# Attention loops of a language-model tower: the turn of the probabilities placed ahead of the V products on TensorE

## What is computed

```python
# banded, four times
idx = jnp.arange(nc)[:, None] * W + jnp.arange(3 * W)[None, :]
scores = jnp.einsum('bhcqd,bhckd->bhcqk', qc, kb) / jnp.sqrt(jnp.asarray(d, q.dtype))
scores = jnp.where(allowed, scores, jnp.asarray(-1000000000.0, scores.dtype))
probs = jax.nn.softmax(scores, axis=-1)
out = jnp.einsum('bhcqk,bhckd->bhcqd', probs, vb)
...
# full, once
attn = jnp.einsum('bhqd,bhkd->bhqk', q, k) * SCALE
attn = jax.nn.softmax(attn, axis=-1)
out = jnp.einsum('bhqk,bhkd->bhqd', attn, v)
```

## Time and profile before

| what | value |
|---|---|
| median of three runs | 1809.26 us |
| the profiled execution, its own time | 1813.13 us |
| its span, first to last instruction | 1811.3 us |
| mean granted TensorE clock | 0.902 |
| busy: TensorE, VectorE, ScalarE, GpSimd | 81%, 68%, 54%, 45% |
| banded loops (four) | 52 to 210, 300.5 to 445, 535.5 to 682, 775 to 921 us |
| full loop | 1334 to 1487 us |

### The profile page before, as it was taken

One profiled execution on the slowest core, in us unless ns is written; L12 is line 12 of the kernel. 1 busy time (PEld: TensorE's weight loads), 2 busy tenths in 40 slices (PEclk: granted clock), 3 DMA queues, 4 the chain that ended last, 5 costly groups with the idle time before them and its releaser, 6 DMA issues.

```text
span 1811.3 us, 39511 instructions
## 1 busy us (share of the span) xinstructions
PE 1465.9 (81%) x13098; PEld 1256.1 (69%) x13098; DVE 1236.5 (68%) x3514; ACT 980.9 (54%) x2393; POOL 815.2 (45%) x1175
## 2 busy tenths in 40 slices
PE   2789799997998888988989488669478887499991
PEld 2578677786777777877778377269457666499991
DVE  6878876889768896688976722434478886444444
ACT  1578635887348883378843133245258872055550
POOL 7786235773347733378523200145365511145540
PEclk9799999999999999999999678579789996599996
DMA  4644004470026530174800000167345501267765
GB/s 114 163 89 106 1 1 123 105 145 11 1 62 146 115 60 1 25 182 89 226 2 1 14 1 1 47 207 244 115 97 119 102 2 47 102 198 243 239 199 182
DMA packets 144278, 177.87 MB, mean 98 GB/s; under 512 B 22096, under 2 KB 106128, under 8 KB 143952
## 3 DMA queue, kind: packets, MB, share of 16 engines
q1 hardware_dynamic: 136784, 158.18, 34.0%
q0 software_dynamic: 7296, 17.18, 2.8%
HBM read 132.96 MB, written 42.34 MB: 97 GB/s over the span
## 4 chain that ended last, share of the span: by engine, by line
PE 53%; DVE 23%; issue 8%; POOL 8%; DMA 4%; ACT 3%; SPq 1%; POOLq 0%; DVEq 0%; ACTq 0%
PE bank L1498 7%; PE bank L663 7%; DVE ptl L821 4%; PE bank L575 4%; DVE neg_max L814 3%; PE bank L427 3%; PE bank L445 2%; PE bank L1484 2%; PE bank L447 2%; PE bank L446 2%; PE bank L449 2%; PE bank L448 2%; DVE xx L788 2%; PE bank L540 2%; DVE row_b L821 1%
## 5 line engine op out<-in xcount | busy, mean ns | idle before, releaser
L703 ACT ACTIVATE prob<-bank,neg_max 128x192 f32<-128x192 f32 (+1 forms) x960 | 412.6, 440 | 117.5 <-DVE neg_max L814 108.9
L814 DVE TENSOR_REDUCE neg_max<-bank 128x2 f32<-128x384 f32 (+1 forms) x480 | 272.2, 569 | 70.6 <-PE bank L540 69.9
L575 PE MATMUL bank<-ident,prob 128*128 128x128 f32 x1536 | 272.1, 290 | 48.3 <-DVE ptl L821 36.1
L716 ACT ACTIVATE pth<-bank 128x384 f16<-128x384 f32 (+1 forms) x480 | 245.9, 512 | 5.7 <-PE bank L575 5.6
L821 DVE TENSOR_TENSOR ptl<-bank,pth 128x384 f16<-128x384 f32 (+1 forms) x352 | 204.5, 581 | 10.5 <-ACT pth L716 10.0
L575 PEld LDWEIGHTS bank<-ident,prob 128*128 128x128 f32 x1536 | 161.7, 142 | 65.0 <-DVE ptl L821 47.6
L670 ACT ACTIVATE xx<-bank 128x256 fp32r<-128x256 f32 x256 | 96.3, 390 | 176.1 <-PE bank L427 172.6
L540 PE MATMUL bank<-kx,qx 96*128 96x192 bf16 (+1 forms) x960 | 166.8, 255 | 1.4 <-DVE xx L788 1.1
L754 ACT ACTIVATE fbuf<-bank,b 128x512 f32<-128x512 f32 x96 | 66.0, 687 | 165.0 <-PE bank L449 165.0
L596 PE MATMUL bank<-v,pth 128*128 128x33 bf16 x1152 | 137.8, 179 | 21.5 <-DVE ptl L821 18.5
L663 PE MATMUL bank<-w,fbuf 128*128 128x192 f32 x768 | 140.7, 326 | 1.9 <-DVE h L914 1.9
(11 more groups left out here) (304 smaller groups left out, 4644.7 us busy)
## 6 DMA issues: line engine op xcount, KB each, us to landing
xn<-in_e_seg SPq DMA_DIRECT2D x34, 768.0 KB, 6.7
w<-in_e_w SPq DMA_DIRECT2D x23, 576.0 KB, 4.3
qk_rows<-fbuf SPq DMA_DIRECT2D x128, 96.0 KB, 2.3
qx<-qk_rows SPq DMA_DIRECT2D x35, 288.0 KB, 4.1
kx<-qk_rows SPq DMA_DIRECT2D x35, 288.0 KB, 5.9
qk_rows<-w SPq DMA_DIRECT2D x80, 96.0 KB, 2.3
qx<-qk_rows SPq DMA_DIRECT2D x35, 192.0 KB, 4.7
kx<-qk_rows SPq DMA_DIRECT2D x35, 192.0 KB, 5.4
```

The costliest lines, as they stand in the source:

```text
L575: last = nc.tensor.transpose(bank[BT[p % 2]][:, c * P:c * P + P], probs_at(p, banded, c * P, P), ident[:, :])
L703: nc.scalar.activation(probs_at(p, banded, qt * n, n), scores_at(p, n)[:, qt, :], ACT.Exp, bias=neg_max[:, b % 2, hd, qt:qt + 1], scale=1. ...
L716: nc.scalar.activation(high_at(p, banded), bank[BT[p % 2]][:, 0:n], ACT.Copy).then_inc(hi_ready.sem, 1)
L814: nc.vector.tensor_reduce(neg_max[:, b % 2, hd, :], scores_at(p, D if banded else S), AX.X, ALU.max, negate=True).then_inc(max_ready.sem, 1)
```

## The change

In every turn of the attention loops the turn of pair p-3 is now issued directly behind the scores of pair p, and the V products of the older pair behind the turn, ahead of `pe_step`. All four banded loops and the full loop go through this function. Nothing else is different: the waits, the buffers and the other engines' programs are the same.

```diff
             for p in range(PAIRS + behind(banded)):
                 if p < PAIRS:
                     pe_scores(pe, it, p, banded)
-                if p >= behind(banded):
-                    pe_values(pe, it, p - behind(banded), banded)
                 if p == 3:
                     pe.wait_ge(y_read.sem, y_read.at(it, 0))
                 if 0 <= p - 3 < PAIRS:
                     pe_turn_probs(pe, it, p - 3, banded)
+                if p >= behind(banded):
+                    pe_values(pe, it, p - behind(banded), banded)
                 pe_step(pe, it, p, banded, w, w_out, tile, xx)
```

## The result

The changed kernel takes 1823.36 us (median of 13 runs, 1816.40 to 1832.02), the kernel before in the same comparison 1808.28 us (13 runs, 1800.30 to 1814.60). The ratio is 1.0081, 95% interval 1.0059 to 1.0103: 0.8% slower, some 15 us, where 19.5 us had been forecast, inside the range.

The account below looks back on a forecast made before the run. A ring from turn over step, scores, maximum and low part was taken to bound the banded loops, no engine being full. 28.2 lost less 8.7 swallowed gave 19.5 us, on 1809.26 rounded 1829 us; range 1812 to 1846 us.

Parts of the forecast that it names:

- The ring, and the V products outside it: Banded loops: turn, step, scores, maximum and low part touch, 2.55 us a lap; V products fill TensorE's wait outside it.
- The lap: Banded loops: one round from turn to turn, covering two pairs, grows from 2.55 to 2.85 us.
- 94 places at 0.30 us, 28.2 us: Banded loops: VectorE's maximum waits for scores 94 times; each pays the V products' 0.30 us issue whole, 28.2 us.
- 8.7 us swallowed by the wait for keys: Banded loops: TensorE's four waits for a later sequence's keys shrink by what was lost, taking 8.7 us off.
- No gain from the earlier turn: Banded loops: only ScalarE's high part (L716) wants the earlier turn; gain at most 5.6 us, taken as 0.
- Full loop at 0: Full loop: V products and turn await the same low part and exchange places within the same 0.69 us; 0.
- The sum: Whole kernel: 28.2 - 8.7 = 19.5 us slower, 1829 us, 1.1%.
- The signs: Changed profile: L814's wait for L540 grows some 28 us, banded loops 4 to 7 us longer each, full loop within 1 us.
- The clock: Attention loops: taken as 0; granted clock below 0.99 would refute the forecast; rival of a falling clock 1869 us, chance 0.04.
- The rule of the Trainium skill: TensorE: frequent short idle spells between matmul groups can swing the clock between two levels, so more loss than the sum.

Follow-up runs that it names:

- the v and out steps out of the ring: Changed kernel's order, with each v or out step issued behind the next pair's scores; 1803.15 us against 1813.14 for the kernel before, ratio 0.9959.
- the kernel with even turns alone: Kernel before, with V products behind the turn only in even loop turns of the banded loops; 1817.64 us, ratio 1.0060.
- three of nine products: Kernel before, with three of the nine V products put behind the turn in the banded loops; 1814.48 us against 1806.62, ratio 1.0048.
- the kernel with all steps late: Kernel before, with every step issued behind the next pair's scores; 1793.36 us, ratio 0.9900.
- The kernel before, once more: The kernel before, run again unchanged against itself; ratio 0.9995 (0.9967 to 1.0024).
- all three kernels with a late step: V and out steps behind the next scores, in the order before (0.9925) or the changed order (0.9959), and every step so in the order before (0.9900).
- the late v and out steps: Kernel before, order kept, with only v and out steps issued behind the next pair's scores; 1797.42 us, ratio 0.9925.

## Why the prediction was right

- **The ring, and the V products outside it.** Shown. The lap grew from 2.55 to 2.87 us (2.85 forecast) where the turn waits for the low part; the products' issue time sets the loss of a lap (2.70 us for three); nearly all of the loss comes from even loop turns; and with the v and out steps out of the ring it is nearly gone in their laps.
- **94 places at 0.30 us, 28.2 us.** The right mechanism, too large. The fourth loop lost 5.3 us, not the 6.6 that its 22 places would give; four times that is 21.2. Two of the 22 are not in the ring: the first scores of the loop (2.4 us before and after) and the scores that wait for keys (2.8 us, which shrank). The other twenty grew by 5.1 us together, 0.26 each: ten by the 0.32 us that nine products take behind the turn or a little more, four by 0.25 to 0.28, six by 0.16 or less. The count should have left out the two, and not every other place pays whole; what covers a part in the six was not looked into. All four loops of the profile give 18.4 us longer and 8.3 less wait for keys, 26.7, of which up to 5.6 are the late openings and the two pauses.
- **8.7 us swallowed by the wait for keys.** Right: 0.4 us of it is left, and the fourth loop shows the 2.2 us given back at its place. In the kernel with even turns alone 3.5 us of the wait were left, and with three of nine products it was 10.3, so the term moves by some us between profiles.
- **No gain from the earlier turn.** Right: ScalarE's 5.6 us before L716 did not change. VectorE's wait for the high part fell from 10.0 to 7.2 us; no shorter lap was seen with it.
- **Full loop at 0.** Nearly: +1.4 us in the profile, from V products that take 0.09 us longer behind transposes. That V products and turn exchange places without cost was assumed, and is not quite so.
- **The sum.** 21.2 - 8.3 + 1.4 = 14.3 us by the fourth loop taken four times, against 14.7 by the ratio (0.0081 x 1808; 10.7 to 18.6 by its interval) and 19.5 forecast. So the forecast is a third too large, clear of noise, by the term of 28.2. That the profiled execution was 18.9 us longer, nearly the forecast, is luck: it was the slowest of its 13, with late openings and pauses that the forecast didn't have.
- **The signs.** The wait of L814 for L540 grew by 22.9 us, not 28. The loops were to be 4 to 7 us longer each and are 0.5, 7.5, 7.2 and 3.1; the full loop was to stay within 1 us and grew by 1.4.
- **The clock.** A granted clock below 0.99 was named as a sign of being wrong. It is 0.97 and 0.96 in the second and third loop, which had 0.99 both; in the fourth and the full loop it is 0.99, as before. But the unchanged kernel, run again, has 0.95 in its third loop too, so the fall isn't tied to the change by these runs. Whether the longer pauses had a part in it was not tried.

The rule of the Trainium skill that spoke against the change, in "TensorE: Matmul & The Clock Gate", Part 1 on the second failure mode, is not borne out by the fourth loop, where the weight loads of the turn waited 30.5 us for low parts instead of 15.3 and the clock stayed at 0.99. The second and third loop neither bear it out nor exclude it.

## What to carry to other kernels

When several engines hand work round and none is full, look for the ring whose links touch, and write down which blocks of an in-order engine stand in it and which stand in its waits. Moving a block of filler from the wait to behind the instruction that waits costs its whole issue time in the laps where every link touches (here 0.32 us), even though the same instructions run; moving a block out of the ring (here the step, to behind the next scores) gains the same way. Before moving one, follow its own wait too: the step in front of the turn brought a second ring through its bank with it.

## What the runs showed of the hardware that was not expected

- Twelve small products behind four fp32 transposes took 0.39 us to issue, ahead of them 0.30; nine took 0.32 instead of 0.30, three took 0.17.
- A stage without any tie to the change is some 8 us longer or shorter from profile to profile. Turning the gate's logits, some 235 us behind the last banded loop, one pair of products took 1.86 us in the kernel before and 1.02 us in the kernel with all steps late:

```profile
1150.46 1.86 PE L2154 MATMUL bank<-fbuf,mask 64*4 64x512 f32 x2
```

```profile
1142.13 1.02 PE L2158 MATMUL bank<-fbuf,mask 64*4 64x512 f32 x2
```

The granted clock from 1125 to 1200 us is 0.50 in the kernel before, its lower level of 1.2 GHz. In the kernel with all steps late the products took little more than half the time, and the granted clock in the same stretch of the stage (1117 to 1192 us there) is 0.66. The kernel before, once more, shows the long form too, the changed kernel as well, and of the ten other profiles three; all three kernels with a late step show the short one. The executions fall apart in the same way: of the twelve of the kernel with V products behind even turns seven took 1813.5 to 1817.7 us and five 1826.0 to 1830.5, none between. TensorE is busy for 43 of 75 us in that stretch. Whether the level of the clock there depends on when the stage begins or on chance is open; as 8 us is half of the effect of this change, it is a reason why ratios here need the laps beside them. It also means that of the 1.0% of the fastest kernel, some 0.4% may be this stage, and of the 0.75% of the late v and out steps the larger part; the loops alone, first to last maximum, are 702.8 us together for the fastest and 711.5 for the late v and out steps against 713.8.
